# A graph layer whose results are stored while the edges still stream in: one whole group per step in place of half a group

## The reference

```
agg = segment_sum(edge_attr, dst)            # 200000 x 128 -> 12500 x 128
h   = relu(layernorm(x))
h   = relu([h, agg] @ W1 + b1)
h   = relu(h @ W2 + b2)
h   = h @ W3 + b3
out = x + layernorm(h) * ln_w + ln_b
```

## Time and profile before

| | |
|---|---|
| median of 3 runs | 314.58 us (313.88 to 315.23) |
| the profiled execution's own time | 314.24 us |
| its span | 312.5 us |
| TensorE busy | 278.0 us, 89% |
| VectorE busy | 233.0 us, 75% |
| ScalarE busy | 156.7 us, 50% |
| GpSimd busy | 133.8 us, 43% |
| HBM read, written | 109.92 MB, 6.40 MB |
| mean rate of the DMA engines | 373 GB/s |

### The profile page before, as it was taken

The page is one execution under the profiler, slowest core; times in us unless marked ns, Lnnn a source line. Parts: engine busy times, 40 slices in busy tenths (PEclk is TensorE's granted clock), DMA queues, the critical chain, the costliest instruction groups (busy, mean ns, idle before and its releaser), DMA issues.

```text
span 312.5 us, 12921 instructions
## 1 busy us (share of the span) xinstructions
PE 278.0 (89%) x3955; PEld 180.8 (58%) x3955; DVE 233.0 (75%) x879; ACT 156.7 (50%) x413; POOL 133.8 (43%) x203
## 2 busy tenths in 40 slices
PE   2967999999999999999999999999999999999992
PEld 0745666665666666566555656565556565655671
DVE  4955777777878778777778777777787777777754
ACT  1443554555555554545555545545545545455533
POOL 7735244444444434344444443344444433444510
PEclk9979999999999999999999999999999999999998
DMA  7999999999999999999999999999999999999996
GB/s 243 341 379 373 373 372 371 373 376 383 383 384 383 384 382 384 382 383 383 383 383 383 384 383 383 382 383 383 383 382 383 382 383 383 383 382 383 382 389 223
DMA packets 83285, 116.50 MB, mean 373 GB/s; under 512 B 7116, under 2 KB 83272, under 8 KB 83272
## 3 DMA queue, kind: packets, MB, share of 16 engines
q1 hardware_dynamic: 82368, 116.06, 104.0%
q10 hardware_dynamic: 904, 0.28, 0.4%
HBM read 109.92 MB, written 6.40 MB: 372 GB/s over the span
## 4 chain that ended last, share of the span: by engine, by line
SPq 46%; PE 21%; issue 15%; DVE 9%; DMA 4%; ACT 3%; ACTq 0%; DVEq 0%
SPq L344 24%; SPq L381 17%; PE part_ps L500 7%; PE place_ps L511 5%; SPq L339 3%; PE hid_ps L534 3%; DVE onehot L976 3%; DMA ring<-in_edge_attr 3%; ACT h L739 3%; PE hid_ps L544 3%; DMA dst_i<-in_dst 1%; DVE agg L1068 1%; SPq L391 1%; DVE local L1002 1%; DVE x_mv L957 1%
## 5 line engine op out<-in xcount | busy, mean ns | idle before, releaser
L902 POOL TENSOR_SCALAR place<-iota,rows_at 128x128 f32<-128x128 f32 x130 | 84.4, 650 | 136.7 <-PE place_ps L511 128.1
L500 PE MATMUL part_ps<-ring,onehot 128*32 128x128 f32 x3120 | 111.9, 277 | 8.4 <-DMA ring<-in_edge_attr 3.4
L500 PEld LDWEIGHTS part_ps<-ring,onehot 128*32 128x32 f32 x3120 | 77.4, 109 | 66.9 <-issue 38.1
L1068 DVE TENSOR_TENSOR agg<-place_ps,agg 128x128 f32 x130 | 37.8, 291 | 58.3 <-PE place_ps L511 58.0
L511 PE MATMUL place_ps<-place,part 128*128 128x128 f32 x260 | 63.4, 326 | 3.9 <-ACT part L725 2.5
L976 DVE TENSOR_TENSOR onehot<-iota,local_t 128x768 f32<-128x768 f32 x65 | 62.4, 962 | 0.1
L739 ACT ACTIVATE h<-xs,x_shift,x_rstd 128x128 f32 (+2 forms) x98 | 41.3, 483 | 32.8 <-DVE x_shift L969 32.8
L511 PEld LDWEIGHTS place_ps<-place,part 128*128 128x128 f32 x260 | 39.1, 189 | 30.5 <-issue 22.1
L725 ACT ACTIVATE part<-part_ps 128x128 f32<-128x128 f32 x130 | 34.7, 267 | 24.8 <-PE part_ps L500 24.8
L910 POOL TENSOR_TENSOR xs<-xs,vecs 128x384 f32 (+2 forms) x33 | 33.5, 1015 | 26.8 <-ACT h L739 26.8
L534 PE MATMUL hid_ps<-agg,w1a 128*128 (+2 forms) x64 | 28.8, 532 | 7.3 <-DVE agg L1068 7.3
(11 more groups left out here) (103 smaller groups left out, 204.1 us busy)
## 6 DMA issues: line engine op xcount, KB each, us to landing
ring<-in_edge_attr SPq DMA_DIRECT2D x260, 384.0 KB, 8.3
xs<-in_x SPq DMA_DIRECT2D x32, 192.0 KB, 7.6
out_x<-xs SPq DMA_DIRECT2D x8, 384.0 KB
out_x<-xs SPq DMA_DIRECT2D x96, 24.0 KB
dst_i<-in_dst SPq DMA_DIRECT2D x1, 768.0 KB
out_x<-xs SPq DMA_DIRECT2D x2, 192.0 KB
tail_e<-in_edge_attr SPq DMA_DIRECT2D x1, 192.0 KB, 4.8
out_x<-xs SPq DMA_DIRECT2D x1, 168.0 KB
```

The costliest lines, as they stand in the source:

```text
L500: last = nc.tensor.matmul(part_ps[par_q % 2][s * WIN:(s + 1) * WIN, 0:D], onehot[:, oct_par, first + s, j, :], e[:, s, j * D:(j + 1) * D], ...
L902: nc.gpsimd.tensor_scalar(place[:, par_q % 2, :], iota[:, 0:P], rows_at[:, k:k + 1], None, ALU.is_equal).then_inc(place_ready, 1)
L1068: nc.vector.tensor_tensor(v, place_ps[par_q % 2][:, 0:P], v, ALU.add).then_inc(added, 1)
```

## The change

The pieces become 32 partitions, 48 KB, four to a group (`PIECES = 4`). From step 3 on every step stores one whole group in four pieces, one behind each quad, where it stored half a group. Step i stores group i - 3. So 26 groups go out in steps 3 to 28 in place of 13, and behind the last load stand two pairs (groups 26 to 29) and group 30 in place of eight pairs and two groups. The split of the last group's pieces into uneven parts (`graded`) is gone. The number of store instructions in a step, four, and their places stay, in all steps but the last two, where eight become four.

```
-PIECES = 8
+PIECES = 4
-STORED_EARLY = 13
+LEVEL_ROUNDS = 1
+STORED_EARLY = 2 * (ROUNDS - LEVEL_ROUNDS)
...
-                def store_part(g, k, graded=False):
-
-                    first_p = k * PIECE
+                def store_part(g, k):
+
+                    p0, p1 = k * PIECE, (k + 1) * PIECE
                     if k == 0:
                         sp.wait_ge(out_ready, g + 1)
-                    sizes = (PIECE - 1 - k, 1 + k) if graded else (PIECE,)
-                    for size in sizes:
-                        rows = out[bass.ds(g * CHUNK + first_p * PER, size * PER), :]
-                        sp.dma_start(rows.rearrange("(p j) f -> p (j f)", j=PER),
-                                     xs[first_p:first_p + size, bass.ds(g * CHUNK, CHUNK)]).then_inc(stored, 16)
-                        first_p += size
+                    rows = out[bass.ds(g * CHUNK + p0 * PER, (p1 - p0) * PER), :]
+                    sp.dma_start(rows.rearrange("(p j) f -> p (j f)", j=PER),
+                                 xs[p0:p1, bass.ds(g * CHUNK, CHUNK)]).then_inc(stored, 16)
...
                             if g is not None:
-                                store_part(g, 4 * (1 - par) + k, graded)
+                                store_part(g, k)
...
-                    with sp.Fori(0, ROUNDS - STORED_EARLY) as t:
+                    with sp.Fori(0, LEVEL_ROUNDS) as t:
                         step(2 * t + 1, 1, t)
                         step(2 * t + 2, 0, t + 1)
-                    with sp.Fori(ROUNDS - STORED_EARLY, ROUNDS - 1) as t:
-                        g = t - (ROUNDS - STORED_EARLY)
-                        step(2 * t + 1, 1, t, g)
-                        step(2 * t + 2, 0, t + 1, g)
-                    t, g = ROUNDS - 1, STORED_EARLY - 1
-                    step(2 * t + 1, 1, t, g, graded=True)
-                    step(2 * t + 2, 0, t + 1, g, more_x=False, graded=True)
+                    with sp.Fori(LEVEL_ROUNDS, ROUNDS - 1) as t:
+                        step(2 * t + 1, 1, t, 2 * t - 2 * LEVEL_ROUNDS)
+                        step(2 * t + 2, 0, t + 1, 2 * t - 2 * LEVEL_ROUNDS + 1)
+                    t = ROUNDS - 1
+                    step(2 * t + 1, 1, t, STORED_EARLY - 2)
+                    step(2 * t + 2, 0, t + 1, STORED_EARLY - 1, more_x=False)
```

More of the change, by code:

```diff
@@ L396, in fast, with step @@
                         reload(q, q % RING)
-                    def step(i, par, pairs, g=None, more_x=True, graded=False):
+                    def step(i, par, pairs, g=None, more_x=True):
                         if more_x:
@@ L425, in fast @@
                     singles = TOP - STORED_EARLY - 2 * pairs
-                    sp.wait_ge(stored, 16 * (PIECES * (STORED_EARLY + 1) + pairs + singles + len(TOP_PARTS) + len(LAST_PARTS)))
+                    sp.wait_ge(stored, 16 * (PIECES * STORED_EARLY + pairs + singles + len(TOP_PARTS) + len(LAST_PARTS)))
                 def general():
```

## The result

| | before | changed |
|---|---|---|
| median | 314.69 us (313.88 to 315.23, 4 runs) | 318.52 us (317.81 to 319.29, 4 runs) |
| profiled execution, its span | 314.24, 312.5 us | 319.19, 317.4 us |
| ratio | | 1.0124, 95% interval 1.0106 to 1.0141 |

The change costs 3.8 us. My forecast was 315.4 us; the time lies in the range of 312.6 to 320.0, on the side to which I had given 0.42.

What follows compares the result with a forecast made beforehand. The prediction took the DMA engines' transfer stream as the bound. Stream +1.2 us and tail -0.2 us gave +1.0 on the profiled 314.24, 315.2; with the median's offset it forecast 315.4 us, range 312.6 to 320.0 for 8 in 10.

Steps and rivals of the forecast that it cites:

- The bound and the path: Whole kernel: DMA engines are short, the end follows the last load, and each microsecond of stream growth moves it by one.
- The first half group is free, the second is not: Stream, steps 3 to 28: first half group cost 0.01 us a step; the second +0.045 us, over 26 steps +1.2 us.
- the two ends: Step length: from below 8.89 us at 398 GB/s, -0.10 us; from above 9.24 us at 383 GB/s, +0.245 us.
- half price: Rival on the stream: rate saturates at about 388 GB/s, step 9.12 us, +3.3 - 0.2, 317.5 us; chance 0.17.
- the price of the first half: Stream of the kernel before: its half group a step cost 0.01 us, where its share at 383 GB/s would be 0.257 us.
- The loss that I added for a pipe near its limit: Stream: +0.045 us a step because a pipe driven about 1% under its highest rate must lose a little when reads bunch.
- the room: Stream: the rate could rise from 383 to 398 GB/s, seen in 299 to 301 us; the second half needs 393.5.
- The reason given, a limit on reading that leaves gaps for stores: Stream: reading is limited at 372 GB/s and leaves gaps into which stores fit, as the rate rose by what stores added.
- The rule of the Trainium skill: HBM to SBUF transfers: HBM binds at about 358 GB/s a core, so the added 2.56 MB would take 7.1 us; set aside.
- The instructions, the wait, the uneven split at 0: SyncE's issues hidden by the queue, wait for group i - 3 with three groups' margin, split's loss: each 0; split up to 0.5 us.
- The tail, -0.2 us: Behind the last load: 13 groups leave a tail hidden by compute; last stores find idle engines, gain 0 to 0.35 us.
- The median: Whole kernel: median of the runs shown, 314.58 us, is 0.3 us above the profiled execution, taken into the 315.4 us forecast.

Runs made afterwards that it cites:

- the heap run: Changed kernel's 26 groups stored unevenly: none in steps 3 to 10, one a step in 11 to 18, two in 19 to 26, one in 27 and 28; 327.04 us.
- the blocks: 13 groups in the stream as in the kernel before, each as one whole 192 KB store in every second step; 317.76 us beside 314.21, ratio 1.0115.

## Why the prediction came out as it did

**The bound and the path: right.** The stream of transfers sets when the last load lands, and the rest follows at a fixed distance. The last quad's sums moved from 301.00 to 305.96, the last store's issue from 309.10 to 314.06, both by 4.96 us (1.6 of them ahead of any store), and nothing in the tail gave any of it back. Nor did other instructions become longer with more stores beside them: on the pages the mean of one `output` of VectorE is 363 ns against 362, and that of one of its one-hot products 961 against 962.

**The first half group is free, the second is not: right in kind, wrong in size.** The step of the prediction that failed is the value chosen between the two ends, "+0.045 us a step, 9.04 us or 391.5 GB/s". It measured +0.14 us, 9.12 us, 388 GB/s, so this term is 3.6 us by the length of a step, 3.3 by the trace from end to end, instead of 1.2. What I called *half price* (388 GB/s, 9.12 us a step, 317.5 us) is what happened, and I had given it 0.17. That the total lies in the range is owed to the range's width, not to this choice. The runs show where the choice went wrong. I took the price of the first half as the nearest row, but the price is not a constant with a cliff at 398 GB/s; it bends upward from half a group on: 0.02 us at a half, 0.08 at three quarters, 0.14 to 0.16 at one. The loss that I added for a pipe near its limit was a guess that no row showed, and 391.5 is 1.6% under 398, not about 1%. And the 398 GB/s in the earlier trace rows, which I took as the room, are no room for stores beside full reading. A rate like it appears for a few microseconds wherever a heap of stores goes through: with one whole store a step, 397 GB/s in 161 to 164 us, and 373 in 164 to 170. With whole steps in the window, no stretch of 24 us or more with stores in the stream read more than 389.

**The reason given, a limit on reading that leaves gaps for stores: supported, not proved.** For it stand the rate of 372 to 373 GB/s in every stretch without stores, early in both kernels, late in the heap run and between the blocks, and the run in which the same bytes were reads: 371 GB/s, four times the price. The blocks fit it too: a store can only use the gaps of the microseconds in which it stands beside loads. The gaps do not take a whole group, for the reads themselves slow down, from 3.342 / 8.98 = 372 GB/s with half a group a step to 3.342 / 9.12 = 366 with a whole one. None of this says why extra reads cost twice their share. What inside the engines or at HBM makes the gaps stays open.

**The rule of the Trainium skill.** The page "DMA: Bandwidth & Descriptors", section "Where 436 GB/s comes from", would, as an estimate, have every stored byte paid in full at about 358 GB/s, 7.1 us. The trace has 388 GB/s for 192 us and 3.3 to 3.6 us, less than the estimate by half and about three times my 1.2. The section gets its 358 by halving a stack's rate between two cores, and this kernel runs on one, which the prediction did not say when it set the figure aside.

**The instructions, the wait, the uneven split at 0: right.** SyncE shows no wait for VectorE on a store of the stream, a load still lands 7.8 us after its issue, and the kernel without the split took 314.49 us beside 314.21. What I had not seen is how little room SyncE has: 13 transfers a step fit, 17 do not.

**The tail, -0.2 us: next to nothing.** The last wait did shrink by 0.2 us, but from the last issue to the end it is 3.3 us against 3.4. Taking 2.56 MB of stores out of the tail brought 0.1 us, because the compute chain had covered them.

**The median.** I set the forecast on one profiled execution and took the median as 0.3 us above it. Profiles carry a start that differs between executions, by up to 2.0 us among those with the same program up to step 3 (59.74 to 61.74); reading step 3's start first, and comparing from there, removes it.

## What to carry to other kernels

Where a stream of loads is the bound, stores beside it can be nearly free up to a density and are not beyond it: here half a group a step cost next to nothing (0.02 us) and a whole one 0.14 us. Read the price at the density that you mean to use, since a price read at half of it says little, and a peak rate from a few microseconds full of stores is not room. Spread the stores between the loads rather than in blocks. Move into the stream only as many stores as the tail behind the last load cannot hide; here the tail hid 13 groups completely, and moving them bought 0.1 us for 3.3. And before a loop gets more transfers, look at the time from issue to landing: where it fell from about 8 us to about 5, the issuing engine had become the bound.

## What the hardware showed that I had not expected

- SyncE needs about 0.6 us for a small or large transfer inside a loop with computed addresses (2.43 us for four). At 17 a step the kernel lost 39.6 us with stores, 28.7 with reads and 38.0 with copies.
- One block is dearer than pieces spread over the loads: 192 KB in one transfer cost 0.27 us more than the same group in eight pieces, and one group a step in one block ran at 381 GB/s where four or eight pieces ran at 388 and 389. The rate rises only while the block goes through, 389 GB/s for 6 us, with 372 to 373 on either side.
- 0.098 MB a step of extra reads in pieces of 16 partitions cost 0.56 us, twice what their bytes take at 372 GB/s, and four times what the same bytes cost as stores (0.14 us).
- Halving the number of load transfers at the same bytes (768 KB each instead of 384 KB) changed nothing: 314.51 us beside 314.46.
